# A graph network on one core: equal edges looked for over 416 places in place of 288, and two blocks of extra rows in place of three

## The chip, the cores and the metric

One NeuronCore of a Trainium2 chip. The metric is the device time of one execution in microseconds (us). The engines are TensorE (PE, its weight loads are listed as PEld), VectorE (DVE), ScalarE (ACT), GpSimd (POOL) and SyncE (SP, which issues DMAs here).

## What is computed

Four graph layers on 6250 nodes of 128 features, with 106,250 edges (50,000 random ones, their reverses and one loop for each node) that come sorted by target. Every layer ends in a residual sum and a layer norm. What matters here:

```python
# layer 0, three times: h is replaced by a GRU cell of the summed messages
m = h @ weight[i]
agg = segment_sum(m[src], dst, num_segments=n_nodes)
h = gru_cell(agg, h, w_ih, w_hh, b_ih, b_hh)
# layer 1: a hypergraph convolution, nodes to hyperedges and back
e_feat = B_inv[:, None] * segment_sum(h[row], col, num_segments=num_edges)
out = D_inv[:, None] * segment_sum(e_feat[col], row, num_segments=num_nodes)
# layer 2: attention over the edges of a source
attn = ee / maximum(denom[src], 1e-16)
out = segment_sum(attn[:, None] * mapped[dst], src, num_segments=N)
# layer 3: an MLP on both ends of each edge, summed at its target
edge_new = _mlp(concatenate([x[src], x[dst]]), We1, be1, We2, be2)
agg = segment_sum(edge_new, dst, num_segments=N)
```

The first three layers sum over the same edges, five times forward or backward and once with attention weights. The kernel makes these sums products with a dense matrix that holds how many edges lead from each node to each node.

## The kernel before, in words

**The matrix.** It stands in DRAM (`adj_t`, and turned over in `adj_s`) as float16 counts, NP = 6656 columns (targets) in 13 groups of GW = 512, and 52 row blocks of 128 in 13 turns of KT = 4 blocks. The 6250 nodes fill NB = 49 blocks. The other three (EXT_BLOCKS, columns EXT to NP, the last three of the last group) are extra columns: a target's run of edges is cut into pieces of RUN = 289, and each piece after the first gets an extra column of its own, which is added back by treating it as an extra row block. Line 65 makes sure that the extra columns suffice for any edges: (E - 1) / 289 is at most 384.

**The preparation.** The edges lie in SL = 8 slabs of 128 partitions by SLW = 104. A scatter cannot add, so edges that fall into the same cell must be found: of such edges one writes the count and the others write elsewhere. For each slab DVE compares every edge's key with the keys of the next HALO = 288 edges (`same_keys`, line 2449). One instruction (line 2456) compares SHIFTS = 12 shifts, so there are TRIES = 24 of them, with four buffers `eq`. For each try PE adds the results up in PSUM (`same_keys` of PE, lines 2086 to 2095): three wide adds of 4 x 104 columns count the equal edges behind each edge, and twelve narrow adds of 104 columns, each shifted by one more column, mark the edges that have an equal one ahead. The narrow adds reach KEYS = 104 + 288 = 392 columns of one PSUM bank, which has 512. `turns` (line 148) writes the first four tries out with constant addresses and puts the others into a loop, in which the narrow adds' columns come from the loop's register. What reaches past a slab is carried to the next (`spill`, line 2557, and the products of lines 2101 to 2104 with the shift matrices `back`; `fwd` brings the next slab's keys, `halo`, line 2047). POOL writes these matrices (lines 1614 to 1629), one instruction each. Then DVE works out the cells of the slab and increments `cells_ready`.

**The scatter.** POOL waits for `cells_ready` of a slab (line 1713) and scatters its cells with 104 indirect DMAs (line 1692), slab after slab. The cells of the last two slabs are laid out anew in four pieces. After each unit `slab_done` is incremented, in the order of the targets.

**Behind the search** DVE, PE and ACT go on with the rest of the preparation (counts, ranks, the first layer's input). Each engine's work is a program in order, and `end_stage` (line 372) holds SP, ACT, PE and DVE until all four are there.

**The passes.** The first pass (`first_sp`, `first_act`, `first_pe`, `first_dve`, lines 590 to 763) reads the matrix as soon as a group is scattered: SP waits for `slab_done` (line 603), and loads tiles of 4 blocks by 512 columns. PE turns each tile over (line 674, 16 transposes) and multiplies it: two products for each block, with the upper and the lower bits of the rows (lines 666 and 667). The order of the groups is 0 to 10, then 12; the rows of the extra blocks are known only then, and 12 short turns add their products (`rows_behind`, line 694, three blocks); group 11 comes last (line 712), because the last edges are in it. Passes 1 to 4 (`matrix_pe`, mode "fm", lines 842 to 893) go through group 12 first, then 0 to 11, again with two products of 512 columns for each block (lines 884 and 886). ACT and DVE each convert half of a tile, and in passes 1 to 3 DVE also sums weighted columns (line 1039). In group 12, the extra columns are known after block 48, and DVE takes them over (`keep_ext`, line 1021) before blocks 49 to 51 go on with 128 columns. Pass 5 is the attention (mode "att"): ACT and DVE make weighted tiles (lines 775 and 1051), and PE has four products of 130 columns for each block (line 891). Beside pass 5 POOL gathers rows of the table (line 1158) that pass 5 writes group by group; the first 18 pairs of rows may start after the third or sixth group, the other 34 pairs after the whole table.

**Behind pass 5** come the edges of layer 3, fed by POOL's gathers.

Of the kernel before, what the change touches and what calls it, by code (L numbers as in the profile page):

```python
# [20 lines left out]
P = 128  # L21
N = 6250
E = 106250
NB = (N + P - 1) // P
NBP = 52
NP = NBP * P
# [4 lines left out]
EC = 832  # L31
E_FULL = E // EC
CH = 8
# [13 lines left out]
W = 132  # L47
# [12 lines left out]

RUN = 289
HALO = RUN - 1
EXT = NB * P
EXT_BLOCKS = NBP - NB
assert (E - 1) // RUN <= NP - EXT
GROUPS = 13
# [10 lines left out]
KT = 4  # L77
# [10 lines left out]
SLE = P * SLW  # L88
SHIFTS = 12
TRIES = HALO // SHIFTS  # L90
BACK = [min(SLW, HALO - d * SLW) for d in range(-(-HALO // SLW))]
assert HALO % SHIFTS == 0 and TRIES % 4 == 0 and RUN > SLW and SL * SLE == P * EC

# [62 lines left out]
def gnn(nc, d):  # L156
    ctx = ExitStack()
    with ctx:
# [90 lines left out]
        mask = edge_b[5][:, 0:EC // 4].bitcast(U8)  # L249
        KEYS = SLW + HALO  # L250
        keyx = stage[:, NBP * W - SL * KEYS:NBP * W].rearrange("p (s c) -> p s c", s=SL)
# [43 lines left out]
        tr_w = stage[:, 10 * P:16 * P].rearrange("p (m f) -> p m f", f=P)  # L295
        carry_row = stage[0:1, 16 * P:16 * P + SL * P + 1]
        carry_in = stage[0:1, 16 * P + SL * P + 1:16 * P + SL * P + 1 + 4 * P]
        assert 16 * P + SL * P + 1 + 4 * P <= NBP * W - SL * KEYS

# [362 lines left out]
        def first_pe(pe):  # L662
# [31 lines left out]
            def rows_behind(n, g, before, turn, i):  # L694
                landed(pe, turn, 0, i, LOOPED)
                turn_over(turn, LOOPED * i, REST)
                wait(pe, S("group_out"), len(FIRST_ORDER) + n - 1 + LOOPED * i)
                pe.wait_ge(S("cast_act"), turn + 1 + LOOPED * i)
                if n == 0:
                    pe.wait_ge(S("ext_kept"), 1)  # L700
                out = psum_fm(0, len(FIRST_ORDER) + n)[:, 0:P if n == len(FIRST_ORDER) - 1 else GW]
                for m in range(1, KT):
                    last = products(out, turn % RING, NB + m - 1, m, m == 1, m == KT - 1)
                last.then_inc(S("tile_used"), 1)
# [6 lines left out]
            wait(pe, S("group_out"), 2 * len(FIRST_ORDER) - 1)  # L711
            tiles_of(2 * len(FIRST_ORDER), LAST_FROM, 0, NBP)

# [128 lines left out]
        def matrix_pe(p, pe):  # L842
            mode = MODES[p]

            def body(n, g, first_turn, i):
                wait(pe, S("group_out"), groups_before(p) + n - 1 + LOOPED * i)
                for t in range(TURNS):
# [4 lines left out]
                    if p == SCALED and n == 0 and t == 10:  # L852
# [7 lines left out]
                        last.then_inc(S("pair_flipped"), 1)  # L860
                    for m in range(KT):
                        k = KT * t + m
# [18 lines left out]
                        if mode == "fm":  # L881
                            tile = tile_r[s][:, m * GW:(m + 1) * GW]
                            cut = P if n == 0 and k >= NB else GW
                            nc.tensor.matmul(psum_fm(p, n)[:, 0:cut], upper_rows[:, k, :], tile[:, 0:cut],  # L884
                                             start=k == 0, stop=False, skip_group_check=True)
                            last = nc.tensor.matmul(psum_fm(p, n)[:, 0:cut], lower_of(p)[:, k, :], tile[:, 0:cut],  # L886
                                                    start=False, stop=k == NBP - 1, skip_group_check=True)
                            continue
                        tile = tile32[s][:, m * GW:(m + 1) * GW]
                        for j in range(1 if n == 0 and k >= NB else KT):  # L890
                            last = nc.tensor.matmul(psum_nm(p, n, j), tile[:, j * P:(j + 1) * P], stage_nm[:, k, 0:AW],  # L891
                                                    start=k == 0 and j % 2 == 0, stop=k == NBP - 1, skip_group_check=True)
                    last.then_inc(S("tile_used"), 1)
# [717 lines left out]
        def _(pool):  # L1611
# [11 lines left out]
            step(nc.gpsimd.memset(ones[:, :], 1.0))  # L1623
            step(nc.gpsimd.memset(rows[:, :, :], 0.0))
            step(nc.gpsimd.iota(slabs(ee), pattern=[[SLE, SL], [1, SLW]], base=0, channel_multiplier=SLW,
# [378 lines left out]
        def _(pe):  # L2004
# [70 lines left out]
            for n in range(SL):  # L2075
# [5 lines left out]
                pe.wait_ge(S("same_ready"), TRIES * n + 1)  # L2081
                opened(4 + n % 2, 4 * SLW)
                if n == 0:
                    opened(6, KEYS)

                def same_keys(i, n=n):
                    for u in range(4):
                        r = 4 * i + u
                        pe.wait_ge(S("same_ready"), TRIES * n + r + 1)
                        for m in range(0, SHIFTS, 4):  # L2090
                            added(4 + n % 2, slice(0, 4 * SLW), ident_h[:, :], eq[u][:, m:m + 4, :].rearrange("p m c -> p (m c)"))
                        for m in range(SHIFTS):
                            last = added(6 + n % 2, bass.ds(SHIFTS * r + m + 1, SLW), ident_h[:, :], eq[u][:, m, :])
                        last.then_inc(S("same_used"), 1)
                turns(pe, TRIES // 4, same_keys)
                if n == 0:
                    extra_sums(0, 1, 5)
                pe.wait_ge(S("spill_ready"), n + 1)
                if n < SL - 1:
                    opened(6 + (n + 1) % 2, KEYS)  # L2100
                for k, w in enumerate(BACK):
# [220 lines left out]
        def _(dve):  # L2322
# [220 lines left out]
            for n in range(SL):  # L2543
# [12 lines left out]
                dve.wait_ge(S("same_used"), TRIES * (n + 1))  # L2556
                nc.vector.tensor_copy(spill, ps[:, 6 + n % 2, SLW:KEYS]).then_inc(S("spill_ready"), 1)
                after = ps[:, 4 + n % 2, 0:4 * SLW].rearrange("p (m c) -> p c m", c=SLW)
# [433 lines left out]
```

## Time and profile before

| What | us |
|---|---|
| median of 3 runs | 4486.95 |
| lowest and highest run | 4484.71, 4487.19 |
| the profiled execution | 4479.83 |
| its span, first to last instruction | 4478.1 |
| PE busy | 3802.7 (85%) |
| DVE busy | 3343.8 (75%) |
| POOL busy | 2568.6 (57%) |
| ACT busy | 2336.8 (52%) |
| mean granted TensorE clock | 0.927 of 2.4 GHz |

Busy shares are means over stages that have different limits. The stages in order: the preparation until 698 us, the first pass until 1217, the GRU steps with passes 1 and 2 until 2213, pass 3 until 2532, pass 4 until 2896, norms and scores, pass 5 from 3054 to 3697, the edges and the output until 4478.

### The profile page before, as it was taken

The page shows a single profiled execution, that of the slowest core. Times are in us where ns is not written, and L with a number is a line of the kernel's source. Part 1 is how long each engine was busy: PE and PEld are TensorE (multiplying, and loading weights), DVE is VectorE, ACT ScalarE, POOL GpSimd, SP SyncE. Part 2 cuts the span into 40 slices and gives each one's busy share as a digit, 9 for nine tenths or more (in the row PEclk, how much of TensorE's full clock was granted, in tenths as well). Part 3 has the DMA queues.
Part 4 walks back from the last instruction along what each step waited for, and adds up shares of the span by engine and source line. Part 5 has one row for each costly group of instructions (what it writes and reads, how often), then busy time and mean ns, then how long its engine had stood idle before and what let it go on. Part 6 is the DMA issues. An engine that isn't in the chain of part 4 may idle for free. (4 is left out here: it accounts for less than half of the span.)

```text
span 4478.1 us, 86002 instructions
## 1 busy us (share of the span) xinstructions
PE 3802.7 (85%) x24420; PEld 3172.3 (71%) x24481; DVE 3343.8 (75%) x7908; ACT 2336.8 (52%) x3120; POOL 2568.6 (57%) x2609
## 2 busy tenths in 40 slices
PE   5888508998889998999599799968999998888876
PEld 3666306776667776877478578748999997777775
DVE  6877897997888888887777643366888777776765
ACT  0000304665555555554455555557888875656655
POOL 3777777777377777777760000000056777777772
PEclk8999758999999999999799899969999998999998
DMA  9930007998828863885288888603566766777863
GB/s 381 373 112 1 3 0 262 366 372 307 284 65 280 271 211 108 293 277 176 91 288 297 190 276 293 231 0 119 158 208 221 247 204 212 245 234 230 260 221 123
DMA packets 372190, 950.50 MB, mean 212 GB/s; under 512 B 114634, under 2 KB 138300, under 8 KB 365251
## 3 DMA queue, kind: packets, MB, share of 16 engines
q1 hardware_dynamic: 225090, 656.12, 44.5%
q10 hardware_dynamic: 58609, 180.13, 10.5%
q0 software_dynamic: 88208, 110.81, 8.7%
q8 instruction: 136, 2.23, 0.2%
q14 instruction: 147, 1.20, 0.1%
HBM read 704.02 MB, written 242.80 MB: 211 GB/s over the span
## 5 line engine op out<-in xcount | busy, mean ns | idle before, releaser
L1752 POOL DMA_INDIRECT edges_halves<-local,gather_idx x832 | 853.0, 1025 | 306.5 <-issue 253.2
L1692 POOL DMA_INDIRECT adj_t<-cell_val,cell_at x832 | 815.9, 981 | 320.5 <-issue 320.5
L884 PE MATMUL ps<-tiles_r,stage_r 128*128 128x512 f32 x2028 | 809.3, 399 | 43.5 <-ACT tiles_r L817 32.9
L1158 POOL DMA_INDIRECT x_fm<-table,gather_idx x288 | 310.1, 1077 | 831.4 <-DMA table<-cell_at 691.8
L817 ACT CAST tiles_r<-onehot 128x1024 fp32r<-128x1024 f16 x338 | 355.1, 1051 | 298.9 <-DMA onehot<-adj_t 158.1
L884 PEld LDWEIGHTS ps<-tiles_r,stage_r 128*128 128x128 f32 x2028 | 385.4, 190 | 145.3 <-issue 26.5
L722 DVE TENSOR_SCALAR_CACHE_REDUCE big<-ps 128x512 f16<-128x512 f16 (+2 forms) x724 | 430.3, 652 | 73.5 <-PE ps L674 62.5
L891 PE MATMUL ps<-stage,big 128*128 128x130 f32 x4046 | 466.6, 277 | 18.1 <-DVE big L1051 15.2
L891 PEld LDWEIGHTS ps<-stage,big 128*128 128x128 f32 x4046 | 461.3, 193 | 18.8 <-issue 14.9
L775 ACT ACTIVATE big<-big,cols,stage 128x512 f32 (+1 forms) x508 | 371.7, 803 | 68.3 <-PE ps L891 53.5
L886 PE MATMUL ps<-tiles_r,lower_r 128*128 128x512 f32 x1016 | 400.7, 394 | 0.0
L886 PE MATMUL ps<-tiles_r,lower_late 128*128 128x512 f32 x1012 | 399.8, 395 | 0.0
L1255 PE MATMUL ps<-big,stage 128*128 x1920 | 263.4, 294 | 100.8 <-ACT stage L1204 41.6
L1290 DVE TENSOR_TENSOR stage<-ps,big 128x128 f32<-128x128 f32 x960 | 202.8, 282 | 179.4 <-PE ps L1255 97.9
L1255 PEld LDWEIGHTS ps<-big,stage 128*128 128x128 f32 x1920 | 241.2, 204 | 128.6 <-issue 128.5
L1061 DVE CAST tiles_r<-onehot 128x1024 fp32r<-128x1024 f16 x338 | 246.1, 729 | 109.5 <-PE ps L886 96.3
L2072 PE MATMUL ps<-big,ident_h 128*128 128x104 bf16 (+1 forms) x2880 | 319.1, 248 | 9.2 <-issue 8.6
L1158 POOL DMA_INDIRECT big<-table,gather_idx x272 | 261.9, 963 | 87.2 <-issue 81.7
L1158 POOL DMA_INDIRECT stage<-table,gather_idx x272 | 259.5, 954 | 82.9 <-issue 81.1
L884 PE MATMUL ps<-rows_r,stage_r 128*128 128x512 f32 x676 | 269.4, 399 | 37.6 <-ACT rows_r L817 36.0
L2072 PEld LDWEIGHTS ps<-big,ident_h 128*128 128x128 bf16 x2880 | 228.6, 101 | 101.4 <-issue 16.9
L622 ACT CAST tiles_r<-onehot 128x2048 fp32r<-128x2048 f16 (+2 forms) x91 | 162.5, 1789 | 253.2 <-DMA onehot<-adj_t 225.5
(511 smaller groups left out, 8418.5 us busy)
## 6 DMA issues: line engine op xcount, KB each, us to landing
onehot<-adj_t SPq DMA_DIRECT2D x332, 512.0 KB
big<-adj_t SPq DMA_DIRECT2D x332, 512.0 KB
onehot<-adj_s SPq DMA_DIRECT2D x170, 512.0 KB
adj_t<-rows ACTq DMA_DIRECT2D x13, 6656.0 KB
adj_s<-big ACTq DMA_DIRECT2D x157, 512.0 KB
big<-edge_rows SPq DMA_DIRECT2D x120, 512.0 KB
big<-adj_s SPq DMA_DIRECT2D x84, 512.0 KB
x_fm<-adj_s SPq DMA_DIRECT2D x84, 512.0 KB
```

Of the source, the lines that this page charges most:

```text
L722: last = nc.vector.tensor_scalar(turned[turn % RING][:, j, of, :].rearrange("p m c -> p (m c)"), flips[turn % 2][:, j, of, :].rearrange("p ...
L775: nc.scalar.activation(tile32[s][:, m * GW:(m + 1) * GW], r_rows[:, bass.ds(g * GW, GW)], ACT.Relu, bias=col(MINUS_ONE), scale=stage_nm[:, ...
L817: nc.scalar.copy(tile_r[s][:, 0:TW // 2], raw_tile(p, s)[:, 0:TW // 2]).then_inc(S("cast_act"), 1)
L884: nc.tensor.matmul(psum_fm(p, n)[:, 0:cut], upper_rows[:, k, :], tile[:, 0:cut], start=k == 0, stop=False, skip_group_check=True)
L886: last = nc.tensor.matmul(psum_fm(p, n)[:, 0:cut], lower_of(p)[:, k, :], tile[:, 0:cut], start=False, stop=k == NBP - 1, skip_group_check= ...
L891: last = nc.tensor.matmul(psum_nm(p, n, j), tile[:, j * P:(j + 1) * P], stage_nm[:, k, 0:AW], start=k == 0 and j % 2 == 0, stop=k == NBP - ...
L1061: nc.vector.tensor_copy(tile_r[s][:, TW // 2:TW], raw_tile(p, s)[:, TW // 2:TW]).then_inc(S("cast_dve"), 1)
L1158: nc.gpsimd.indirect_dma_start(to[:, u * P:(u + 1) * P], None, table[0:N, :], bass.IndirectOffsetOnAxis(gather_idx[:, r:r + 1], 0)).then_i ...
L1255: last = nc.tensor.matmul(spot.q_bank(g)[:, (u % 4) * P:(u % 4 + 1) * P], ring_ohT[:, h * CH + u, :], q_nm[:, bass.ds(blk[u] * P, P)], sta ...
L1692: nc.gpsimd.indirect_dma_start(out, bass.IndirectOffsetOnAxis(cells[:, c:c + 1], 0), cell_val[:, c:c + 1], None).then_inc(S(name), 16)
L1752: nc.gpsimd.indirect_dma_start(edges_halves, bass.IndirectOffsetOnAxis(slot_at[:, at:at + 1], 0), slot_val[:, at:at + 1], None).then_inc(h ...
L2072: return nc.tensor.matmul(ps[:, bank, of], stationary, moving, start=False, stop=True, skip_group_check=True)
```

## The change

RUN becomes 417, so at most 254 extra columns are needed, and two blocks hold them (LIVE = 51 blocks). The third extra block stays in the layout of the matrix, but its products are left out: as rows (block 51) and, in the group of the extra columns, as its last 128 columns. The search goes over 416 edges: 13 shifts in a try, 32 tries. KEYS grows to 520, 8 more than a PSUM bank has, so the last four tries are written out with constant addresses (`last_one`), and the columns past the bank are added to a free part of the counting bank (OVER = 8). Four shift matrices of a kind are needed in place of three. A row that stood in `stage` moves to `rows`, of which only the half that must be zero is filled.

```diff
-RUN = 289
+RUN = 417
...
-assert (E - 1) // RUN <= NP - EXT
+LIVE = NBP - 1
+assert (E - 1) // RUN <= LIVE * P - EXT
...
-SHIFTS = 12
+SHIFTS = 13
 TRIES = HALO // SHIFTS
+KEYS = SLW + HALO
+BANK = 512
+OVER = max(KEYS - BANK, 0)
...
-        carry_row = stage[0:1, 16 * P:16 * P + SL * P + 1]
...
+        carry_row = rows[:, :, :].rearrange("p t w -> p (t w)")[0:1, TW // 2:TW // 2 + SL * P + 1]
...
-                for m in range(1, KT):
-                    last = products(out, turn % RING, NB + m - 1, m, m == 1, m == KT - 1)
+                for m in range(1, 1 + LIVE - NB):
+                    last = products(out, turn % RING, NB + m - 1, m, m == 1, m == LIVE - NB)
...
-            tiles_of(2 * len(FIRST_ORDER), LAST_FROM, 0, NBP)
+            tiles_of(2 * len(FIRST_ORDER), LAST_FROM, 0, LIVE)
...
-                    for m in range(KT):
+                    for m in range(min(KT, LIVE - KT * t)):
...
-                            cut = P if n == 0 and k >= NB else GW
+                            cut = GW if n else P if k >= NB else GW - (NBP - LIVE) * P
...
-                        for j in range(1 if n == 0 and k >= NB else KT):
+                        for j in range(KT if n else 1 if k >= NB else KT - (NBP - LIVE)):
...
-            step(nc.gpsimd.memset(rows[:, :, :], 0.0))
+            step(nc.gpsimd.memset(rows_flat[:, 0:TW // 2], 0.0))
...
-                opened(4 + n % 2, 4 * SLW)
+                opened(4 + n % 2, 4 * SLW + OVER)
                 if n == 0:
-                    opened(6, KEYS)
+                    opened(6, KEYS - OVER)
...
-                def same_keys(i, n=n):
+                def same_keys(i, n=n, last_one=False):
                     for u in range(4):
                         r = 4 * i + u
                         pe.wait_ge(S("same_ready"), TRIES * n + r + 1)
                         for m in range(0, SHIFTS, 4):
-                            added(4 + n % 2, slice(0, 4 * SLW), ident_h[:, :], eq[u][:, m:m + 4, :].rearrange("p m c -> p (m c)"))
+                            to = min(m + 4, SHIFTS)
+                            added(4 + n % 2, slice(0, (to - m) * SLW), ident_h[:, :], eq[u][:, m:to, :].rearrange("p m c -> p (m c)"))
                         for m in range(SHIFTS):
-                            last = added(6 + n % 2, bass.ds(SHIFTS * r + m + 1, SLW), ident_h[:, :], eq[u][:, m, :])
+                            over = SHIFTS * r + m + 1 + SLW - BANK if last_one else 0
+                            if over > 0:
+                                added(4 + n % 2, slice(4 * SLW, 4 * SLW + over), ident_h[:, :], eq[u][:, m, SLW - over:SLW])
+                                last = added(6 + n % 2, slice(BANK + over - SLW, BANK), ident_h[:, :], eq[u][:, m, 0:SLW - over])
+                            else:
+                                last = added(6 + n % 2, bass.ds(SHIFTS * r + m + 1, SLW), ident_h[:, :], eq[u][:, m, :])
                         last.then_inc(S("same_used"), 1)
-                turns(pe, TRIES // 4, same_keys)
+                turns(pe, TRIES // 4 - 1, same_keys)
+                same_keys(TRIES // 4 - 1, last_one=True)
...
-                nc.vector.tensor_copy(spill, ps[:, 6 + n % 2, SLW:KEYS]).then_inc(S("spill_ready"), 1)
+                nc.vector.tensor_copy(spill[:, 0:HALO - OVER], ps[:, 6 + n % 2, SLW:KEYS - OVER])
+                nc.vector.tensor_copy(spill[:, HALO - OVER:HALO], ps[:, 4 + n % 2, 4 * SLW:4 * SLW + OVER]).then_inc(S("spill_ready"), 1)
```

## Rows read from the trace of the kernel before

**Rows 1.** The chain that ended last, its shares by line.

```profile
by line: PE ps L891 13.2%; POOL big L1158 5.3%; POOL stage L1158 4.9%; issue 4.4%; DMA edge_rows<-big 0.9%; PE ps L2265 0.5%; DMA edge_rows<-stage 0.4%; POOL edge_rows L1137 0.4%; PE ps L2272 0.3%; PE ps L909 0.3%; PE ps L2252 0.2%; DVE big
```

**Rows 2.** Busy time by stretch: length; PE, PEld, DVE, ACT, POOL; clock, DMA share, GB/s.

```profile
266.00:467.00 201.00, 170.40 (x1519) 123.20 (x1519) 158.31 (x176) 0.00 (x0) 152.84 (x159) 0.93 0.02 1
541.00:670.00 129.00, 0.40 (x2) 0.43 (x2) 128.27 (x258) 0.00 (x0) 98.01 (x102) 0.50 0.02 0
740.00:1040.00 300.00, 298.25 (x2520) 239.47 (x2520) 271.84 (x902) 200.58 (x112) 228.09 (x237) 1.00 1.01 369
1145.00:1176.00 31.00, 27.00 (x215) 20.22 (x216) 29.90 (x104) 16.23 (x11) 21.57 (x23) 1.00 0.91 276
```

**Rows 3.** PE's adds in order of time (start, us, what); last, line 2072's durations.

```profile
179.71 6.82 PE L2072 MATMUL ps<-big,ident_h 128*128 128x416 bf16 x60 [0.28 <-issue]
186.86 6.79 PE L2072 MATMUL ps<-big,ident_h 128*128 128x416 bf16 x60 [0.32 <-issue]
...
187.91 0.59 PE L2072 MATMUL ps<-big,ident_h 128*128 128x104 bf16 x4
...
223.34 1.02 PE L2072 MATMUL ps<-big,ident_h 128*128 128x416 bf16 x13
...
228.67 1.59 PE L2072 MATMUL ps<-big,ident_h 128*128 128x416 bf16 x13
...
L2072 PE MATMUL ps<-big,ident_h x2880: 210/217/554, 32.0 to 461.0; 128*128 128x416 bf16 x192
```

**Rows 4.** Slab 3 in order of time: DVE's first compares, its copy behind, PE's spill.

```profile
215.35 16.46 DVE L2456 TENSOR_TENSOR big<-ps,stage 128x1248 bf16<-128x1248 f32 x12
...
258.96 0.46 DVE L2557 COPY big<-ps 128x288 f32<-128x288 f32 x1 [5.64 <-PE ps L2072]
...
259.66 1.46 PE L2072 MATMUL ps<-big,onehot 128*128 128x104 f32 x12
```

**Rows 5.** POOL's shift matrices and scatters: durations in ns, first and last start.

```profile
L1619 POOL TENSOR_SCALAR_AFFINE_SELECT onehot<-ident x12: 286/297/1718, 1.2 to 13.1; 128x128 f32<-128x128 f32 x12
...
L1692 POOL DMA_INDIRECT adj_t<-cell_val,cell_at x832: 963/968/1823, 86.4 to 1168.6; - x167
```

**Rows 6.** PE in the first pass, in order of time.

```profile
1019.50 0.40 PE L674 MATMUL ps<-ident_c,onehot 128*128 128x128 f16 x4
...
1054.57 0.40 PE L674 MATMUL ps<-ident_c,onehot 128*128 128x128 f16 x4
...
1066.85 1.86 PE L674 MATMUL ps<-ident_c,big 128*128 128x128 f16 x16 [11.36 <-DMA big<-adj_t]
...
1145.09 0.55 PE L708 MATMUL ps<-ident,big 128*128 128x128 f32 x3 [1.42 <-DVE big L753]
...
1178.37 1.74 PE L674 MATMUL ps<-ident_c,onehot 128*128 128x128 f16 x16 [1.75 <-DVE acc L744]
...
1216.49 0.40 PE L667 MATMUL ps<-tiles_r,lower_r 128*128 128x512 f32 x1
```

**Rows 7.** Stretches of passes 1 and 3, and waits in the first groups of passes 1 to 3.

```profile
1353.00:1425.00 72.00, 72.00 (x309) 58.76 (x309) 64.57 (x157) 38.85 (x37) 55.54 (x55) 0.98 0.87 286
2290.00:2500.00 210.00, 210.00 (x914) 171.40 (x914) 150.03 (x339) 120.72 (x115) 35.64 (x34) 1.00 0.88 296
...
DVE big L1024 <- PE ps L886: 3.5, 1, 3.5
DVE big L1024 <- PE ps L886: 4.9, 1, 4.9
DVE big L1024 <- PE ps L886: 5.2, 1, 5.2
```

**Rows 8.** The chain in pass 5 (start, us, what); POOL's first gather behind the pass.

```profile
3230.92 39.31 PE ps L891 x352
...
3699.94 1.72 POOL L1158 DMA_INDIRECT big<-table,gather_idx  x1 [4.58 <-DMA table<-cell_at]
```

More of the change, by code:

```diff
@@ L88 @@
 SLE = P * SLW
-SHIFTS = 12
+SHIFTS = 13
 TRIES = HALO // SHIFTS
+KEYS = SLW + HALO
+BANK = 512
+OVER = max(KEYS - BANK, 0)
 BACK = [min(SLW, HALO - d * SLW) for d in range(-(-HALO // SLW))]
-assert HALO % SHIFTS == 0 and TRIES % 4 == 0 and RUN > SLW and SL * SLE == P * EC
+assert HALO + SLW - SHIFTS <= BANK and 4 * SLW + OVER <= BANK and HALO % SHIFTS == 0 and TRIES % 4 == 0 and RUN > SLW and SL * SLE == P * EC
 ZEROED = [(GROUPS - 1, 0, 1), (2, 3, 4, 5), (6, 7, 8, 9, 10, 11)]
@@ L249, in gnn @@
         mask = edge_b[5][:, 0:EC // 4].bitcast(U8)
-        KEYS = SLW + HALO
         keyx = stage[:, NBP * W - SL * KEYS:NBP * W].rearrange("p (s c) -> p s c", s=SL)
@@ L295, in gnn @@
         tr_w = stage[:, 10 * P:16 * P].rearrange("p (m f) -> p m f", f=P)
-        carry_row = stage[0:1, 16 * P:16 * P + SL * P + 1]
-        carry_in = stage[0:1, 16 * P + SL * P + 1:16 * P + SL * P + 1 + 4 * P]
-        assert 16 * P + SL * P + 1 + 4 * P <= NBP * W - SL * KEYS
+        carry_row = rows[:, :, :].rearrange("p t w -> p (t w)")[0:1, TW // 2:TW // 2 + SL * P + 1]
+        carry_in = stage[0:1, 16 * P:16 * P + 4 * P]
+        assert 16 * P + 4 * P <= NBP * W - SL * KEYS and TW // 2 + SL * P + 1 <= 2 * CH * W
         extra_to, first_dst, extras, extra_base, extra_ends, last_dst = [slab_f[:, k, :] for k in range(6)]
@@ L886, in body @@
                             last = nc.tensor.matmul(psum_fm(p, n)[:, 0:cut], lower_of(p)[:, k, :], tile[:, 0:cut],
-                                                    start=False, stop=k == NBP - 1, skip_group_check=True)
+                                                    start=False, stop=k == LIVE - 1, skip_group_check=True)
                             continue
                         tile = tile32[s][:, m * GW:(m + 1) * GW]
-                        for j in range(1 if n == 0 and k >= NB else KT):
+                        for j in range(KT if n else 1 if k >= NB else KT - (NBP - LIVE)):
                             last = nc.tensor.matmul(psum_nm(p, n, j), tile[:, j * P:(j + 1) * P], stage_nm[:, k, 0:AW],
-                                                    start=k == 0 and j % 2 == 0, stop=k == NBP - 1, skip_group_check=True)
+                                                    start=k == 0 and j % 2 == 0, stop=k == LIVE - 1, skip_group_check=True)
                     last.then_inc(S("tile_used"), 1)
@@ L2099, in _ @@
                 if n < SL - 1:
-                    opened(6 + (n + 1) % 2, KEYS)
+                    opened(6 + (n + 1) % 2, KEYS - OVER)
                 for k, w in enumerate(BACK):
```

## The prediction

> **What bounds the kernel now.** I read the chain of waits first: 13.2% of it is matmuls of line 891, the attention pass, and some 10% is POOL's gathers of line 1158 behind that pass [rows 1]. It is cut off at its early end, so the front half has to be read by stages. In busy time by stage the reader should see three different limits [rows 2]. From 266 to 467 us, where equal cells are looked for, neither PE (170 of 201 us) nor DVE (158) is full; from 541 to 670 DVE alone works (128 of 129 us); from 740 to 1040, in the first pass, PE has 298 of 300 us. The instructions in order of time settle the search. In its loop PE starts a turn of four tries (60 adds) at 179.71 and the next at 186.86: 7.15 us a turn, 1.79 us a try [rows 3]. DVE's compares run at 16.46 / 12 = 1.37 us a try for as long as buffers are free, and at the end of a slab DVE stands 5.64 us idle until PE is done [rows 4]. So **PE's adds set the search**, at 258.96 - 215.35 = 43.6 us a slab. They are not bound by columns: in the unrolled first turn 13 adds take 1.02 us, in the loop 1.59, with four narrow ones in 0.59 us, or (0.59 - 0.217) / 3 = 0.124 us from start to start (0.217 is the median of one) [rows 3].
>
> POOL scatters slab after slab without a pause from 86.4 to 1168.6 us, 832 times [rows 5], slower than slabs are found. It is late only for the end of the first pass: PE goes through a group there in 1054.57 - 1019.50 = 35.07 us, stands still for 11.36 us before group 10 is scattered, and for 1.75 us at the last group [rows 6].
>
> **Part 1: the search.** There are 32 tries in place of 24, each with 17 adds in place of 15 (one more of a single shift, and a fourth wide one that is only 104 columns). A loop turn has a fixed part that stays. The narrow add costs 0.124 us in the loop. The short fourth wide one lies between 0.05 us (its address is a constant, like those of the unrolled turn: 1.02 us less one add's 0.217, over 12, is 0.067) and 0.124; I take 0.055, nearest to the constant case. A try is longer by 0.18 us, a turn by 0.72: 7.15 becomes 7.87.
> - Five looped turns get longer: 5 x 0.72 = 3.6 us. One more looped turn: 7.9.
> - The last turn is unrolled now, and 8 of its adds are split in two. Nothing of before shows an unrolled last turn. At the pace of the unrolled first turn (0.067 an add) its 76 adds cost 5.1 us, at the loop's pace 76 x 0.124 = 9.4. The addresses are constants, so I take 5.5.
> - First turn: 8 more adds at 0.067, 0.5 us. Sum: 17.5 us a slab.
> - Around it: the carried part is copied in two pieces, 120 columns more (0.3 us with the second instruction), the halo copy grows by 128 columns (0.13), and the spill has two more float32 products of what took 1.46 us for twelve instructions, four of them 0.49 [rows 4]. The two more halo products run beside DVE's 5 us of cell arithmetic and cost nothing; without that cover, 0.5 us. Together 0.9.
>
> A slab is 18.4 us longer, eight are **147 us**. POOL writes four more shift matrices at a median of 0.297 us before PE's first sum [rows 5]: 1 us, with the shorter fill of the zero rows set against its gaps. So the preparation ends 148 us later, and in full, because what follows the search on DVE is a serial string that waits for no load (128 of 129 us busy [rows 2]). The POOL queue: only slab 0 holds the scatters back, by 18.4 + 1 = 19 us, so that they end near 1188; later slabs come every 69 us, against 104 scatters in 1168.6 - 86.4 = 1082 us over 8 = 135 us.
>
> **Part 2: the first pass** starts 148 us later, and its waits for POOL go, since the scatters shift by 19 us only. What is won back: the 11.36 us; groups 10 and 12 took 1066.85 to 1143.67 (1145.09 less its 1.42 of waiting), 76.8 us in place of 2 x 35.07, so 6.7; the last group's 1.75 and its slower start (38.5 us from 1178.37 to 1216.89, against 36.8 in 13 turns of 2.83, a 35.07 group being twelve such turns and a short one), 1.7 [rows 6]. That is 21.5 us. The products left out behind the groups (two of six in each of 12 turns) bring nothing: from 1145 to 1176 DVE is busy 29.9 of 31 us with turning tiles and adding rows [rows 2], and that work stays; if DVE were faster they would bring 12 x 0.46 = 5.5. In the last group two products go, 0.46 us. The stage ends 148 - 22 = **126 us later**.
>
> **Part 3: passes 1 to 4.** A 512-column product takes 210 / 914 = 0.230 us where PE is always busy [rows 7]. Twelve groups lose two each: 5.5 us a pass where PE sets the pace. In passes 1 and 2 DVE also weighs tiles and is busy 64.57 of 72 us [rows 7], so less than the whole arrives: 4 us each; passes 3 and 4 get 5.5. In the first group 98 products shrink from 512 to 384 columns, a quarter of 0.230 or 0.058 each: 5.6 us at most. There DVE waited 3.5, 4.9 and 5.2 us for PE in passes 1 to 3 before it took the extra block [rows 7]; that wait caps the gain, as DVE's casts are next. I take 3, 4.5, 5.5 and 5. Together 19 + 18 = **37 us**; with every product at full price it would be 45, and with tiles landing no sooner than now perhaps 15.
>
> **Part 4: the attention pass.** A product is 39.31 / 176 = 0.2234 us (352 in the row are two instructions each) [rows 8]. Twelve groups lose four: 10.7 us; the first loses one of four in 49 blocks and one of the last block, 50 x 0.2234 = 11.2. But POOL's early gathers run beside the pass, held by the sixth group's rows, which come only 11.2 + 5 x 0.89 = 15.6 us sooner, and POOL had 4.58 us to spare at the end [rows 8]. So of 21.9 us, 15.6 + 4.6 = **20** arrive; the gathers behind are unchanged.
>
> **Sum.** 126 - 37 - 20 = +69 us, on the profiled execution's 4479.83 (span 4478.1 and 1.7 around it) 4549. The runs' median, 4486.95, lies 7.1 us above that execution; against it the forecast is **4556 us**. Differences under 0.2% (9 us) cannot be told from none here.
>
> **Rivals.**
> - **Adds at the unrolled pace.** If a looped add cost what an unrolled one does, 17 adds would take 1.14 us and DVE's compares would set the search: grown with its columns 1.37 x 1352 / 1248 = 1.48 us a try [rows 4], 32 x 1.48 + 3 = 50 us a slab, 7 more than now. The preparation grows by 8 x 7.9 + 1 = 64 us, and 64 - 22 - 57 = -15: **4472, faster**. It decides at a growth of (22 + 57 - 1) / 8 = 9.8 us a slab. Against it: the loop turn, now at 7.15 us where this pace would give DVE's 4 x 1.37 = 5.5. The Trainium skill, TensorE: Matmul & The Clock Gate, section Back-to-back issue gap, has a rule of this kind: a warm matmul starts N / 2.4 + 2.5 ns after the one before, an estimate of 46 ns at 104 columns. By that rule the search would be DVE's; the trace disagrees, with 124 ns in the loop. Chance 0.05.
> - **The products are worth less.** If the tiles' loads pace passes 1 to 4 as soon as PE is quicker (their DMA share is 0.87 to 0.88 already [rows 7]), the gain there is 15 us and not 37: **4578**. For it: in pass 1 DVE has little left. Against it: in the first pass the same queues move 369 GB/s [rows 2] against 296 in pass 3. Chance 0.14.
> - **A dearer search.** The last turn at the loop's pace (9.4 for 5.5) and the wide add at 0.124 (32 x 0.07 = 2.2): 6 us a slab more, 48 in all: **4604**. The constant addresses speak against it. Chance 0.08.
> - **Nothing to see.** A slab's growth near 10 us and the rest as above, **4487**; nothing in the rows gives that. Chance 0.03.
> - That the change leaves nothing out is no rival: the loops over blocks have fixed counts, whatever the edges are.
>
> **How the numbers follow.** The forecast has 0.70; all but the first and the fourth rival are slower. The low end allows 16.5 us a slab (-15), the full price of all products (-10) and a little of the waits; the high end takes in the second rival and a third of the third: 4528 to 4592. Slower by over 0.2%: 0.70 + 0.14 + 0.08 = 0.92; within 0.2%: 0.03; faster: 0.05.
>
> **What would show it.** Right: a loop turn of 68 adds near 7.9 us and a slab near 61; the first tile load of the first pass near 847 us; no wait of PE for a group in it, with 35.07 us a group; its end near 1343; passes of 23.2 us a group; gathers behind the attention pass as many and as long. Wrong: compares back to back through a slab (first rival), gaps for loads in each group of passes 1 to 4 (second), a last turn above 8 us (third). If POOL still holds the last group, part 2 is wrong.

## The result, and the profile after

Over the runs of both kernels on one chip the median went from 4485.83 to **4552.69 us**, a ratio of **1.0157** (95% interval 1.0134 to 1.0181): slower by 67 us. The forecast was 4556, in a range of 4528 to 4592. The profiled execution of the changed kernel took 4554.65 us, its span 4552.9, so the two spans differ by 74.8 us; the stages below add up to 71.6 of it, and the rest lies between them. The medians differ by less because the profiled execution of the kernel before was 6.0 us faster than its median, and that of the changed kernel 2.0 us slower. One execution of the kernel before with its search written out (experiment 3) took 7646.51 us and is left out of the ratio given there.

| Stage (us) | before | after | difference | predicted |
|---|---|---|---|---|
| first pass starts (PE) | 702.9 | 839.2 | +136.3 | +148 |
| first pass, length | 514.0 | 498.3 | -15.7 | -22 |
| passes 1 to 4, lengths | 331.4, 325.7, 318.0, 325.4 | 329.1, 321.2, 309.5, 309.6 | -2.3, -4.5, -8.5, -15.8 | -7, -8.5, -11, -10.5 |
| attention pass, length | 631.6 | 613.7 | -17.9 | -20 arriving |
| end | 4478.1 | 4552.9 | +74.8 | +69 |

**The search** in order of time: TensorE in slab 3 of the changed kernel (start, us, what), which answers to [rows 3] and to the last line of [rows 4].

```profile
271.12 0.54 PE L2071 MATMUL ps<-rows,ident_h 128*128 128x424 bf16 x1 [5.38 <-DVE big L2466]
271.45 14.32 PE L2075 MATMUL ps<-big,ident_h 128*128 128x416 bf16 x136
286.04 7.39 PE L2075 MATMUL ps<-big,ident_h 128*128 128x416 bf16 x68 [0.27 <-DVE big L2466]
293.70 7.38 PE L2075 MATMUL ps<-big,ident_h 128*128 128x416 bf16 x68 [0.27 <-issue]
301.35 7.37 PE L2075 MATMUL ps<-big,ident_h 128*128 128x416 bf16 x68 [0.27 <-issue]
309.03 7.33 PE L2075 MATMUL ps<-big,ident_h 128*128 128x416 bf16 x68 [0.32 <-issue]
316.66 12.57 PE L2075 MATMUL ps<-big,ident_h 128*128 128x416 bf16 x144 [0.30 <-issue]
330.20 1.93 PE L2075 MATMUL ps<-big,onehot 128*128 128x104 f32 x16 [0.97 <-DVE big L2568]
```

A looped turn of 68 adds takes 301.35 - 293.70 = 7.65 us, where one of 60 took 7.15. The last piece is one more looped turn of 7.65 and the unrolled last turn of 76 adds, so 12.57 - 7.65 = 4.9 us for the latter. One part of the profile hints at why a looped add is dear. The view of one source line lists what ran for it on each queue (durations in ns: least, median, most). First the line of the adds in the kernel before, then in the changed one:

```profile
L2072 PEldq FUSED_REGOPS  x1920: 46/46/79, 36.9 to 460.9; - x192
```

```profile
L2075 PEldq FUSED_REGOPS  x2496: 46/46/79, 40.0 to 593.2; - x192
```

2496 is 8 slabs x 6 turns x 4 tries x 13, and 1920 is 8 x 5 x 4 x 12: one register instruction for each narrow add of the loop, whose column comes from the loop's register, and none for any other add. Experiment 2 tests whether they are the cost.

**The first pass**: PE's first and last groups in order of time. The third to fifth line are three of the twelve short turns with the rows behind; the sixth opens the last group, the seventh the stage behind. [Rows 6] are the same places before.

```profile
839.20 1.86 PE L677 MATMUL ps<-ident_c,onehot 128*128 128x128 f16 x16 [17.47 <-DMA onehot<-adj_t]
...
1228.50 1.05 PE L677 MATMUL ps<-ident_c,big 128*128 128x128 f16 x16 [0.20 <-DVE big L725]
...
1275.64 0.51 PE L669 MATMUL ps<-rows_r,stage_r 128*128 128x512 f32 x1 [0.61 <-DVE acc L747]
1278.15 0.50 PE L669 MATMUL ps<-tiles_r,stage_r 128*128 128x512 f32 x1 [0.62 <-DVE acc L747]
1280.65 0.50 PE L669 MATMUL ps<-tiles_r,stage_r 128*128 128x512 f32 x1 [0.64 <-DVE acc L747]
...
1298.22 1.89 PE L677 MATMUL ps<-ident_c,onehot 128*128 128x128 f16 x16 [1.85 <-DVE acc L747]
...
1349.97 1.22 PE L2196 MATMUL ps<-acc,w_late 128*128 128x256 f32 x2 [12.43 <-SPq L380]
```

The 11.36 us before group 10 are gone. But the twelve short turns have a period of 2.51 us where it was 2.59, now with a gap of 0.6 us in each, and the wait ahead of the last group is still there (1.85 for 1.75), for DVE. POOL's scatters end where they were expected (forecast 1188):

```profile
L1695 POOL DMA_INDIRECT adj_t<-cell_val,cell_at x832: 963/967/1857, 105.7 to 1187.3; - x167
```

**Passes 1 to 4**, each from its first product to its last, busy times (columns as in [rows 2]):

```profile
1446.90:1776.00 329.10, 313.10 (x1329) 250.65 (x1329) 279.32 (x677) 176.45 (x168) 253.75 (x248) 0.98 0.85 276
1871.10:2192.40 321.30, 308.65 (x1329) 248.87 (x1329) 271.00 (x651) 176.31 (x168) 246.92 (x245) 0.99 0.87 282
2329.90:2639.30 309.40, 307.24 (x1329) 252.35 (x1329) 220.93 (x495) 176.48 (x168) 93.57 (x87) 0.98 0.86 292
2679.70:2989.40 309.70, 307.46 (x1345) 253.17 (x1345) 134.66 (x212) 176.55 (x169) 0.00 (x0) 0.98 0.86 294
```

PE is full in passes 3 and 4 and idle for 16 and 13 us in passes 1 and 2, where DVE has 279 and 271 us of work. **Behind the attention pass** POOL's first late gather waits 3.32 us; before it was 4.58 [rows 8], so the early gathers did not hold the pass back.

```profile
3773.47 1.73 POOL L1161 DMA_INDIRECT big<-table,gather_idx  x1 [3.32 <-DMA table<-cell_at]
```

### The profile page after: what moved, and what is told of

Same layout as the page of the kernel before. It is cut to its first block and busy times, and to the rows that moved or that the text cites. A ratio compares the mean times of both kernels' runs of the same rounds, so it can differ in the third digit from the quotient of the medians.

```text
span 4552.9 us, 89238 instructions
## 1 busy us (share of the span) xinstructions
PE 3863.6 (85%) x25682; PEld 3226.4 (71%) x25751; DVE 3465.3 (76%) x7980; ACT 2332.7 (51%) x3120; POOL 2558.2 (56%) x2613
## 5 line engine op out<-in xcount | busy, mean ns | idle before, releaser
L887 PE MATMUL ps<-tiles_r,stage_r 128*128 128x512 f32 (+1 forms) x1989 | 788.6, 397 | 51.0 <-ACT tiles_r L820 43.4
L894 PE MATMUL ps<-stage,big 128*128 128x130 f32 x3898 | 453.2, 278 | 18.9 <-DVE big L1054 15.9
L894 PEld LDWEIGHTS ps<-stage,big 128*128 128x128 f32 x3898 | 447.8, 194 | 19.6 <-issue 12.6
L2075 PE MATMUL ps<-big,ident_h 128*128 128x104 bf16 (+3 forms) x4416 | 444.9, 241 | 12.0 <-issue 10.4
L2466 DVE TENSOR_TENSOR big<-ps,stage 128x1352 bf16<-128x1352 f32 x256 | 392.5, 1563 | 52.3 <-PE ps L2075 51.3
L2075 PEld LDWEIGHTS ps<-big,ident_h 128*128 128x128 bf16 x4416 | 326.7, 100 | 131.8 <-issue 24.5
L889 PE MATMUL ps<-tiles_r,lower_late 128*128 128x512 f32 (+1 forms) x993 | 389.4, 392 | 0.0
L889 PE MATMUL ps<-tiles_r,lower_r 128*128 128x512 f32 (+1 forms) x996 | 388.9, 391 | 0.0
L887 PE MATMUL ps<-rows_r,stage_r 128*128 128x512 f32 (+1 forms) x663 | 263.0, 397 | 38.4 <-ACT rows_r L820 36.8
```

The lines of the kernel that those rows point to most:

```text
L2075: return nc.tensor.matmul(ps[:, bank, of], stationary, moving, start=False, stop=True, skip_group_check=True)
L2466: nc.vector.tensor_tensor(eq[done % 4], own_keys(n).unsqueeze(1).to_broadcast([P, SHIFTS, SLW]), bass.AP(behind.tensor, behind.offset, [be ...
```

## The experiments

**1. The two halves of the change, each alone.** The long search with all products is one edit of the changed kernel; the products left out of the kernel before are the change's lines for PE without those of the search.

```diff
-LIVE = NBP - 1
+LIVE = NBP
```

> The changed kernel with the products of the third block put back (the search stays long). Theory A, from the trace of after: the block is worth what the stages showed, 24 us in passes 1 to 4 (little in passes 1 and 2, nearly the full price in 3 and 4) and 21 in the attention pass, and about 1 us in the first pass, so this kernel takes 4553 + 46 = about 4599 us, 1.025 of before, and passes 1 and 2 are less than 5 us longer each than in the changed kernel. Theory B, the prediction's sizes: 37 + 20 us, 4610, 1.028, with passes 1 and 2 longer by 7 and 8.5 us. Theory C, every product at full price (45 + 22 + 6): 4626, 1.031.

Measured: 4605.04 us, ratio 1.027 (1.0253 to 1.0288). The changed kernel is 52.4 us faster than that, between theory A (46) and the prediction's sizes (57). Stage by stage the products bring 1.8 us in the first pass, 2.4, 5.4, 8.3 and 10.9 in passes 1 to 4, and 23.5 in the attention pass.

```diff
+LIVE = NBP - 1
...
-                    for m in range(KT):
+                    for m in range(min(KT, LIVE - KT * t)):
...
-                            cut = P if n == 0 and k >= NB else GW
+                            cut = GW if n else P if k >= NB else GW - (NBP - LIVE) * P
...
-                        for j in range(1 if n == 0 and k >= NB else KT):
+                        for j in range(KT if n else 1 if k >= NB else KT - (NBP - LIVE)):
```

> The kernel before with the products of its last block left out and its search unchanged (24 tries); it no longer has room for the extra columns that a worse input could bring. Theory A: 24 + 21 us are gained behind the first pass, nothing in it since POOL's scatters and DVE hold its end: 4486 - 45 = 4441, 0.990 of before; the wait of 11 us for a scatter in the first pass stays. Theory B (the prediction's sizes): 4429, 0.987. If the two parts add up, the ratios of this kernel and of the one with the long search alone multiply to about 1.015.

Measured: 4432.60 us, ratio 0.9889 (0.9873 to 0.9906), 53 us faster than the kernel before beside it, nearer to theory B. 1.027 x 0.9889 = 1.0156: the two halves add up, and neither hides in the other. PE's wait for group 10 is where it was:

```profile
1065.52 1.87 PE L675 MATMUL ps<-ident_c,big 128*128 128x128 f16 x16 [11.76 <-DMA big<-adj_t]
```

So the search costs 1.027 x 4485 - 4485, about 120 us, and the products give 52 of it back.

**2. What a looped add costs.** The changed kernel with all eight turns written out:

```diff
-                turns(pe, TRIES // 4 - 1, same_keys)
-                same_keys(TRIES // 4 - 1, last_one=True)
+                for i in range(TRIES // 4):
+                    same_keys(i, last_one=i == TRIES // 4 - 1)
```

> The changed kernel with all turns of TensorE's search loop unrolled, so that each narrow add has a constant address. Theory A (what costs 124 ns is the register address of a looped add, one more instruction for the engine's sequencer): adds run at 0.046 and 0.176 us throughout, DVE's compares set the pace at 1.47 us a try, a slab takes 32 x 1.47 + 3.5 = 50.5 us in place of 60, preparation ends 8 x 9.5 = 76 us sooner, no wait for POOL comes back in the first pass: 4477 us, 0.998 of before, faster than either kernel or level with before. Rival B: the longer code has to be fetched, 68 adds and their weight loads a turn, and TensorE waits for it: no gain, 4553, with gaps of issue between adds. Rival C: the adds wait for each other in the accumulator and only the first and last turn hide it: 4553.

Measured: **4472.41 us, ratio 0.9973 (0.9963 to 0.9984)**, faster than the kernel before. DVE's 32 compares of a slab now run without a gap, one every 1.47 us, and a slab takes 518.77 - 469.92 = 48.9 us (here DVE in the last slab), where the changed kernel takes some 59:

```profile
469.92 47.22 DVE L2466 TENSOR_TENSOR big<-ps,stage 128x1352 bf16<-128x1352 f32 x32
518.77 0.58 DVE L2567 COPY big<-ps 128x408 f32<-128x408 f32 x1 [1.63 <-PE ps L2075]
```

PE follows it, 552 adds in one row of slab 3 with no idle time worth a line of its own, so neither the longer code nor a wait of the adds for each other (rivals B and C) stands in the way:

```profile
243.11 46.86 PE L2075 MATMUL ps<-big,ident_h 128*128 128x416 bf16 x552
```

Unrolling removes two things, the loop and the register address. The next kernel keeps the loop and takes the register alone away, so that its narrow adds reach the columns of the first turn only:

```diff
-                                last = added(6 + n % 2, bass.ds(SHIFTS * r + m + 1, SLW), ident_h[:, :], eq[u][:, m, :])
+                                last = added(6 + n % 2, slice(SHIFTS * u + m + 1, SHIFTS * u + m + 1 + SLW), ident_h[:, :], eq[u][:, m, :])
```

> The changed kernel, its search still a loop of six turns, with each narrow add of the loop at a constant column of the accumulator in place of one worked out from the turn (so the carried counts land in wrong columns). Theory A (the register address costs 124 ns): adds run at 46 and 176 ns inside the loop too, VectorE sets the pace, a slab takes about 50 us as in the fully unrolled search (49.3), some 4475 us in all. Rival B (the loop costs it: its branch and the fetch of its body): a turn stays at 7.65 us, a slab at 60, 4553.

Measured: 4475.36 us in one run (the kernel before beside it: 4481.03), a slab at 48.9 us as in the kernel written out, and no register instruction left on the line (its view lists 4416 adds, as many weight loads, and no FUSED_REGOPS):

```profile
242.65 46.87 PE L2075 MATMUL ps<-big,ident_h 128*128 128x416 bf16 x552
```

Shown: the register address is the cost; the loop itself costs nothing that shows at the pace that DVE sets.

**3. Would the kernel before gain as much?** Its own search loop, written out:

```diff
-                turns(pe, TRIES // 4, same_keys)
+                for i in range(TRIES // 4):
+                    same_keys(i)
```

> The kernel before with its search loop unrolled on TensorE (24 tries, all products). Theory A: the slab falls from 43 to 24 x 1.37 + 3 = 36 us and preparation ends some 58 us sooner, but POOL's scatters, which run without a pause until 1169, end only some 7 us sooner, so TensorE waits that much longer for the tenth group of the first pass (11 us becomes about 60): 4478 us, 0.998 of before. Rival B: the scatters are not what holds the first pass, and the 58 us arrive: 4428, 0.987.

Measured: 4481.97 us, ratio 0.9988 (0.9979 to 0.9998): theory A. The trace is from a further run of the same kernel:

> The kernel before with its search loop unrolled, once more, for its trace. Theory A: a slab near 36 us, the first tile load some 58 us earlier, and TensorE's wait for the tenth group of the first pass 11 + 50 = about 60 us, the first pass ending within 10 us of 1217. Rival B (the scatters do not hold it): the wait stays near 11 us and another place, later in the kernel, has taken the 58 us.

Measured: 4484.27 us in one run. A slab falls to 34.2 us, the first pass starts 51.6 us sooner (651.3), and takes 42.2 us longer; PE's wait for group 10 has grown from 11.36 us to

```profile
1058.90 1.86 PE L674 MATMUL ps<-ident_c,big 128*128 128x128 f16 x16 [44.73 <-DMA big<-adj_t]
```

The scatters end at 1160 instead of 1169, and the first pass ends 9.5 us sooner. So in the kernel before POOL sets that end, and of 52 us saved in the search a fifth gets through the first pass; in the changed kernel the search itself sets it. Passes 1 and 2 of this trace are together 8.8 us longer than in the kernel before, so that little of the fifth is left at the end; why, no run here shows.

**4. Why passes 1 and 2 give so little.** The view of waits names ACT: here pass 2 of the changed kernel (1900 to 2190 us), the waits of PE and ACT, then SP's queue in the same stretch (total us, times, longest).

```profile
ACT tiles_r L820 <- DMA onehot<-adj_t: 60.2, 64, 4.2
...
PE ps L887 <- ACT tiles_r L820: 8.2, 8, 1.4
```

```profile
SPq L149 <- DVE tiles_r L1064: 146.5, 102, 4.7
```

Read from the bottom: SP waits for DVE's cast to free a buffer, so the load is late, so ACT is, so PE is. But with a DMA share of 0.87 the loads could themselves be the limit (the second rival). So DVE's weighing was cut to a quarter of its columns (the sums of weights then lack the other three quarters), in the changed kernel and in the one with all products.

```diff
-                        nc.vector.scalar_tensor_tensor(out, raw_tile(p, (first_turn + t) % RING)[:, m * GW:(m + 1) * GW],
-                                                       1.0, weights_of[n % 2], ALU.mult, ALU.mult,
+                        nc.vector.scalar_tensor_tensor(out[:, 0:P], raw_tile(p, (first_turn + t) % RING)[:, m * GW:m * GW + P],
+                                                       1.0, weights_of[n % 2][:, 0:P], ALU.mult, ALU.mult,
```

> The changed kernel, in which VectorE's weighing of tiles beside passes 1 to 3 reads and writes 128 columns of each 512 (so the sums of weights are of a quarter of the columns). Asked: why the products left out bring little in passes 1 and 2. Theory A: VectorE, which weighs three tiles in two turns there, frees the buffers late, so loads are issued late; with it relieved passes 1 and 2 (329 and 321 us) fall to the 309 us of passes 3 and 4. Rival B: the loads themselves, beside POOL's scatters of sorted edges that run through passes 1 and 2, come no faster (a DMA share of 0.86 to 0.88): both passes stay within 5 us of 329 and 321.

Measured: 4515.94 us in one run, 36.8 below the changed kernel's median. Passes 1 and 2 take 304.7 and 308.8 us, and the same queues now move 297 and 293 GB/s (columns as above):

```profile
1449.20:1753.90 304.70, 302.42 (x1329) 249.40 (x1329) 186.24 (x674) 176.41 (x168) 238.63 (x217) 0.99 0.88 297
1849.30:2158.10 308.80, 306.36 (x1329) 252.99 (x1329) 185.98 (x650) 176.21 (x168) 241.18 (x222) 0.98 0.88 293
```

> The same quarter weighing in the kernel with the long search alone (all products). Theory A: passes 1 and 2 (331.5 and 326.6 us) fall to near the 318 of pass 3, and the difference to the changed kernel with quarter weighing becomes the full price of the products, 8 to 11 us in each of the two passes, in place of 2.4 and 5.4. Rival B: both passes stay, and so do the differences of 2.4 and 5.4.

Measured: 4582.94 us in one run; passes 1 and 2 take 316.8 and 317.3 us, so with DVE relieved the products are worth 12.1 and 8.5 us there, in place of 2.4 and 5.4. Each is a single run, and the same pass of two kernels that do the same in it differs by up to 5 us from trace to trace, so 12.1 and 8.5 are rough; the falls of 24.4 and 12.4 us in the changed kernel are beyond that. The loads are not the limit; DVE is.

**5. A version that uses both findings.** With the search unrolled, ACT casts more of each tile in passes 1 and 2: 5/8 in a first kernel, 3/4 in a second (whose edit is shown), in place of half.

```diff
+        CAST = {p: 3 * TW // 4 if p in (1, 2) else TW // 2 for p in range(6)}
...
-                    nc.scalar.copy(tile_r[s][:, 0:TW // 2], raw_tile(p, s)[:, 0:TW // 2]).then_inc(S("cast_act"), 1)
+                    nc.scalar.copy(tile_r[s][:, 0:CAST[p]], raw_tile(p, s)[:, 0:CAST[p]]).then_inc(S("cast_act"), 1)
...
-                        nc.vector.tensor_copy(tile_r[s][:, TW // 2:TW], raw_tile(p, s)[:, TW // 2:TW]
+                        nc.vector.tensor_copy(tile_r[s][:, CAST[p]:TW], raw_tile(p, s)[:, CAST[p]:TW]
```

> The kernel with the unrolled search, in which ScalarE casts 1280 of a tile's 2048 columns in passes 1 and 2 and VectorE 768, in place of 1024 each. Theory A (VectorE is the bound there: three weighings in two turns at 0.76 us and a cast of 0.695 make 1.83 us a turn, against 8 x 0.230 = 1.84 of TensorE, and the work behind a group comes on top): VectorE is relieved by about 0.17 us a turn, 2.3 us a group, TensorE's waits of 1.3 to 2.3 us a group go, passes 1 and 2 fall from 325 and 323 us to about 311, and the kernel from 4472 to about 4446, 0.991 of before. Rival B: ScalarE, whose cast grows from 1.05 to about 1.31 us behind a load that comes no sooner, is late in VectorE's place: 4472 or more.

Measured: 4451.51 us, ratio 0.9938 (0.9921 to 0.9954). The two passes take 317.4 and 321.2 us, 638.6 together for 648.1 with half: 9.5 us of the 26 that 311 each would give, so a part of the way only. Some 5 us of the gain lie elsewhere, in an attention pass of 608.6 us in place of 614.1 (see the section on why the prediction was right).

> The same with 1536 columns for ScalarE and 512 for VectorE. Theory A: VectorE is relieved by 0.35 us a turn and ScalarE's cast takes about 1.57 of 1.84 us a turn; passes 1 and 2 near 309 if ScalarE keeps up, so 4443; if the load's arrival and that cast together are too long for a ring of four buffers, waits for ScalarE take the place of those for VectorE and it lies between 4446 and 4472. Rival B: ScalarE late, above 4472.

Measured: **4443.99 us, ratio 0.9914 (0.9897 to 0.9931)**, faster than either kernel. Passes 1 and 2 take 308.1 and 312.2 us; ACT has 240 us of work in each and keeps up.

```profile
1364.80:1672.90 308.10, 304.01 (x1329) 248.87 (x1329) 227.54 (x675) 240.39 (x168) 241.88 (x218) 0.99 0.87 293
1768.60:2080.80 312.20, 307.98 (x1329) 252.63 (x1329) 220.77 (x650) 240.10 (x168) 244.18 (x224) 0.98 0.88 289
```

The same two edits in the kernel before, with its short search and all products, tell whether the change is worth having then:

> The kernel before (24 tries, all products) with both other edits: the search loop unrolled and 1536 columns for ScalarE's cast in passes 1 and 2. Asked: is the change worth its longer search once neither TensorE's register addresses nor VectorE in passes 1 and 2 stand in the way. Theory A: the unrolled search brings nothing more than the 0.1% of before, since POOL's scatters hold the first pass; the cast brings passes 1 and 2 from 331 and 326 us to the 318 of pass 3, 20 us: 4482 - 20 = 4462, 0.996, so that the same kernel with the longer search and 51 blocks (4444) is 18 us faster than this one. Rival B: the longer search costs as much as the products bring: this kernel lies at 4444 or below.

Measured: 4460.65 us, ratio 0.9949 (0.9933 to 0.9966). Its first pass waits 44.15 us for group 10. So with both limits out of the way the change itself gains some 16 us (0.9949 - 0.9914 of 4485; the two intervals do not overlap, though only just). With the search alone written out on both sides the two kernels (0.9973 and 0.9988) can hardly be told apart. So the loss of 67 us hung on how the adds are addressed; the gain takes DVE's relief as well.

## Why the prediction was right, and where its terms were not

The sign, the order of size and the cause held: the search pays in full, the products give less than half of it back. That 4556 came so close is partly luck: the search was off by -12 us, the first pass by +6, and at the prices of experiment 1 passes 1 to 4 by +10 and the attention pass by -3.5, and these cancel. (In the pair of traces the last two are off by +6 and +2: the trace of before has a fourth pass some 5 us longer, and an attention pass some 6 us shorter, than the kernel of experiment 1, which does the same work there.)

- **The search, 147 us forecast.** Too dear. From slab to slab (starts of the first compares, slabs 1 to 7) the changed kernel takes 67.5 us where the kernel before took 50.6, so 16.9 more and not 18.4. The step that failed is the short fourth wide add, put at 0.055 us: the eight new adds of a looped turn cost 7.65 - 7.15 = 0.50 us, 0.125 a try, which is the new narrow add alone. What paces the loop is the register instructions, and a wide add needs none. The last turn cost 4.9 us, not 5.5, since an unrolled narrow add takes 0.046 us and not the 0.067 that I took as a mean over narrow and wide. That the last turn is cheap because its addresses are constants was right (experiment 2).
- **The preparation passes its delay on in full**: right; the first pass starts 136.3 us later, 8 x 16.9 and 1 of POOL. (From 541 to 670 us DVE is not alone, as the text has it: POOL's scatters run for 98 of these 129 us [rows 2], but nothing on DVE waits for them.)
- **The first pass, 22 us won back.** The main part was right: from the last group before the wait to the group behind (1054.57 to 1142.75 before, 88.2 us) it now takes 70.4, so 17.8 came back of the 18.1 forecast (11.36 and 6.7). What failed are the last group's 1.75 us and its slow start, 3.45 us in all, which I put down to POOL: [rows 6] already named DVE's line 744, and the wait stands at 1.85 us with POOL long done. Where the releaser that a row named contradicted the story, the row was right. Three middle groups took together 1.6 us more than 3 x 35.05, with short waits for DVE. The products left out behind the groups brought 1.8 us in experiment 1, close to the nothing forecast: DVE's additions keep the turn at 2.51 us.
- **Passes 1 to 4, 37 us.** Experiment 1 gives 27.0. Passes 3 and 4 were right (19.2 of 21.5). The first groups came as forecast: from first product to first product they gained 3.4, 4.8, 5.3 and 5.2 us against 3, 4.5, 5.5 and 5. The step that failed is "4 us each" for the twelve groups behind in passes 1 and 2: they take 25.2 us a group in pass 1 before and 25.3 after, and 24.7 both times in pass 2, no gain at all. (The "23.2 us a group" among the signs does not follow from the prediction's own price: 102 x 0.230 = 23.5, and 23.46 is what a group takes in passes 3 and 4 where nothing waits.) I had read DVE's share in [rows 7] (64.57 of 72 us) as room. In order of time it is none: from the start of a weighing to what follows it are 0.61 to 0.66 us, from that of a cast 0.61 to 0.76, so three weighings and two casts in two turns make some 1.60 us a turn and 20.8 a group, the copy of a finished group 0.7, and at the start of a group DVE waits some 3 us for a load; that is an estimate of 24.5 us, against the 23.5 that PE now needs. Three rows of a turn, and the wait at the start of two groups of pass 1:

```profile
1580.32 0.68 DVE L1042 SCALAR_TENSOR_TENSOR big<-big 128x512 f32<-128x512 f16 x1
...
1580.93 0.73 DVE L1042 SCALAR_TENSOR_TENSOR big<-big 128x512 f32<-128x512 f16 x1
...
1581.59 0.81 DVE L1064 CAST tiles_r<-big 128x1024 fp32r<-128x1024 f16 x1
...
1573.36 0.69 DVE L1042 SCALAR_TENSOR_TENSOR big<-big 128x512 f32<-128x512 f16 x1 [3.31 <-DMA big<-adj_t]
...
1623.16 0.69 DVE L1042 SCALAR_TENSOR_TENSOR big<-onehot,big 128x512 f32<-128x512 f16 x1 [2.95 <-DMA onehot<-adj_t]
```

  My expectation for the smaller shift of the cast made the same kind of slip the other way: it added up lengths of instructions that overlap (1.83 us a turn), where starts give 1.60, and left out the wait: 0.17 us a turn turned out too little and 0.35 enough. What makes the load at the start of a group late (SP issues the group's weights just ahead of it) was not tried.
- **The attention pass, 21.9 at full price, 20 arriving.** It gained 17.9 us in the pair of traces and 23.5 in experiment 1. The cap by POOL's early gathers did not bind: 3.32 us of its waiting were left. The pair of traces is the less typical of the two. In the changed kernel's trace 32 products behind a wait of 2.94 us run at half pace, with a granted clock of 0.53 over these 6.7 us, near the lower of the two levels (1.2 of 2.4 GHz); in the trace of before they run at the full pace behind a wait of 2.82 us. Of the ten other profiled executions of this length nine have the slow products too, and only the one with 5/8 of the cast on ACT does not. Like compared with like, the four executions with all products that have the slow place take 637.2 to 637.9 us and those of 51 blocks 612.9 to 614.1; the two without it take 631.6 (before) and 608.6. Either way the products are worth some 23 us, 3 more than forecast and 1 more than the full price; what adds that 1 was not tried. First the row of the kernel before, then the changed kernel's:

```profile
3494.10 3.83 PE L891 MATMUL ps<-stage,big 128*128 128x130 f32 x32 [2.82 <-issue]
```

```profile
3568.06 6.82 PE L894 MATMUL ps<-stage,big 128*128 128x130 f32 x32 [2.94 <-DVE acc L943]
```

- **The first rival** was wrong as a forecast and right as a price: adds at the unrolled pace would give 4472 us, and the kernel in which they run at that pace takes 4472.41. That it agrees to the microsecond is luck again: its preparation grew by 57.7 us and not 64, and the products gave less than its 57. The Trainium skill, TensorE: Matmul & The Clock Gate, section Back-to-back issue gap, gives N / 2.4 + 2.5 ns from start to start for a matmul by itself, an estimate of 46 ns at 104 columns and 176 at 416. Unrolled turns, in which every add has a weight load of its own, agree with it: one wide add and fourteen of 104 columns take 0.99 us (0.176 + 13 x 0.046 + 0.21 for the last one's own length). The loop does not, with 0.124 us, because a register instruction stands ahead of each narrow add (experiment 2).

```profile
324.54 0.99 PE L2075 MATMUL ps<-big,ident_h 128*128 128x416 bf16 x15
```

- **The second rival** (loads pace passes 1 to 4) saw the small gain of passes 1 and 2 and had the wrong cause: with DVE relieved the loads come at 297 GB/s where they came at 276.

## What to carry to other kernels

Price a matrix product in a loop by how its address is given: with short products a register address can cost more than the product, and writing the loop out may be worth more than any product left out. Before a saving on one engine is counted, add up the other engines' starts and waits over one whole period of the loop; a busy share of 0.9 next to a full engine may leave no room. And when work is shortened ahead of a queue that runs without pause, ask which of the two sets the end: the same unrolling was worth 80 us in one of these kernels and some 3 to 5 in the other.

## What the runs showed of the hardware

A narrow add of 104 columns starts 0.124 us after the one before when its column comes from a register, and 0.046 us after it when the column is a constant, in a loop or out of it; the register instruction itself is listed with 46 ns. In a looped try the first narrow adds still come at the short pace and only the later ones at the long one: eight of them, from the second to the ninth, take

```profile
294.33 0.78 PE L2075 MATMUL ps<-big,ident_h 128*128 128x104 bf16 x8
```

which is (0.78 - 0.218) / 7 = 0.08 us a step, between the two. The register instructions run ahead while the wide adds are at work. In the first half microsecond of that try (293.69 to 294.23) the view of the line lists three wide adds, no narrow one, and already four register instructions:

```profile
L2075 PEldq FUSED_REGOPS  x4: 46/46/65, 293.7 to 294.2; - x4
L2075 PE MATMUL ps<-big,ident_h x3: 339/339/347, 293.7 to 294.1; 128*128 128x416 bf16 x3
```

The thirteen of the try start from 293.7 to 295.3, most of them 0.124 us apart, and the last narrow adds start 0.10 us behind their own. So the register instructions set the length of the try, 1.85 us, and the wide adds fit beside them.

Writing six turns of each slab out made TensorE's code longer by 5 x 68 x 8 = 2720 adds, and no wait for instructions shows at DVE's pace: DVE's compares follow each other without a gap.
